# A fused attention and feed-forward layer on 8 cores: the last tile's order of work around its last norm

## The reference

```python
qkv = x @ W_qkv                      # 16 heads of 64
# rotary embedding, windows of 128 tokens that look back one window, causal mask
attn = softmax(mask(q @ k.T)) @ v
x = layernorm(x + attn @ W_out)
gate, up = x @ w_gate.T / 127, x @ w_up.T / 127      # 3072 hidden, int weights
x = layernorm(x + (silu(gate) * up) @ w_down.T / 127)
```

## Time and profile before

| what | value |
|---|---|
| median of 3 runs | 1616.28 us (1616.17 to 1749.54) |
| the profiled execution's own time | 1617.83 us |
| its slowest core, core 7, first to last instruction | 1616.3 us |
| the other cores' spans | 1605.2 to 1614.8 us |
| TensorE busy | 1558.8 us, 96% of the span |
| VectorE, ScalarE, GpSimd busy | 39%, 31%, 14% |
| HBM read / written | 325.19 / 16.78 MB |
| mean granted TensorE clock, core 7 | 0.987 |

### The profile page before, as it was taken

One profiled execution on the slowest core, in us unless ns is written; L12 is line 12 of the kernel. 1 busy time (PEld: TensorE's weight loads), 2 busy tenths in 40 slices (PEclk: granted clock), 3 DMA queues, 4 the chain that ended last, 5 costly groups with the idle time before them and its releaser, 6 DMA issues.

```text
span 1616.3 us, 24558 instructions; the slowest of 8 cores (1605.2 to 1616.3 us)
## 1 busy us (share of the span) xinstructions
PE 1558.8 (96%) x9152; PEld 743.3 (46%) x9152; DVE 624.3 (39%) x1037; ACT 504.2 (31%) x721; POOL 220.2 (14%) x412
## 2 busy tenths in 40 slices
PE   6789999999999999999999999999999999997998
PEld 2344445544454444544445444554445444453443
DVE  0642316522264233632246322562326523363123
ACT  2532224422343223432234222443224422342110
POOL 5112220011100111011110111101120011100100
PEclk9889999999999999999999999999999999999999
DMA  9999995299833989159871798628974299612861
GB/s 152 204 141 182 183 160 101 56 159 160 138 73 72 176 150 156 41 96 174 148 131 37 134 172 142 110 60 137 168 134 92 53 170 162 105 53 46 141 101 52
DMA packets 83635, 198.87 MB, mean 123 GB/s; under 512 B 11712, under 2 KB 20032, under 8 KB 83520
## 3 DMA queue, kind: packets, MB, share of 16 engines
q0 software_dynamic: 64896, 161.51, 64.3%
q1 hardware_dynamic: 18624, 35.81, 6.1%
HBM read 325.19 MB, written 16.78 MB: 212 GB/s over the span
## 4 chain that ended last, share of the span: by engine, by line
PE 90%; DMA 4%; DVE 2%; ACT 2%; issue 1%; POOL 1%; SPq 0%; DVEq 0%; ACTq 0%; POOLq 0%
PE sc L422 40%; PE dn L342 21%; PE dn L391 7%; PE pvb L255 5%; PE dn L255 5%; PE dn L262 3%; PE pvb L262 2%; DMA gu<-wgu_d 2%; DMA h_sb<-wqk_d 2%; PE sc L255 2%; PE sc L303 2%; PE pvb L322 1%; ACT y_fm L550 1%; PE pvb L369 1%; PE sc L262 1%
## 5 line engine op out<-in xcount | busy, mean ns | idle before, releaser
L422 PE MATMUL sc<-y_fm,gu 128*128 128x512 bf16 x2880 | 645.5, 380 | 6.4 <-DMA gu<-wgu_d 4.8
L422 PEld LDWEIGHTS sc<-y_fm,gu 128*128 128x128 bf16 x2880 | 281.5, 98 | 351.0 <-issue 16.3
L753 DVE TENSOR_TENSOR h_sb<-pt,sc 128x512 bf16<-128x512 bf16 x192 | 132.0, 688 | 676.2 <-PE sc L422 628.9
L342 PE MATMUL dn<-wd,h_sb 128*128 128x512 bf16 x1536 | 345.9, 379 | 2.9 <-ACT y_fm L550 2.9
L576 ACT ACTIVATE pt<-sc,consts 128x512 bf16<-128x512 f32 x192 | 131.9, 687 | 321.2 <-PE sc L422 321.1
L342 PEld LDWEIGHTS dn<-wd,h_sb 128*128 128x128 bf16 x1536 | 144.4, 98 | 171.5 <-issue 4.9
L870 POOL DMA_DIRECT2D gu<-wgu_d x180 | 95.2, 529 | 692.5 <-PE sc L422 659.8
L541 ACT ACTIVATE pt<-sc,consts 128x1024 f16<-128x1024 f32 x112 | 129.7, 1202 | 169.4 <-PE sc L303 169.2
L391 PE MATMUL dn<-wo,attn_fm 128*128 128x512 f16 x512 | 117.7, 383 | 2.6 <-ACT attn_fm L546 2.6
L862 POOL DMA_DIRECT2D qk<-wqk_d x112 | 59.8, 538 | 350.9 <-PE sc L255 227.0
L734 DVE SCALAR_TENSOR_TENSOR r<-dn,consts,y_tm 128x512 f32<-128x512 f32 x64 | 48.1, 751 | 128.7 <-PE dn L342 128.7
(11 more groups left out here) (112 smaller groups left out, 1108.1 us busy)
## 6 DMA issues: line engine op xcount, KB each, us to landing
gu<-wgu_d POOLq DMA_DIRECT2D x180, 512.0 KB, 7.1
qk<-wqk_d POOLq DMA_DIRECT2D x112, 256.0 KB, 7.6
out_tm<-r SPq DMA_DIRECT2D x32, 512.0 KB, 2.8
rotb<-qraw SPq DMA_DIRECT2D x232, 64.0 KB, 5.7
x<-x_fm POOLq DMA_DIRECT2D x16, 512.0 KB, 12.9
xt<-x_tm POOLq DMA_DIRECT2D x30, 256.0 KB, 6.5
wd<-wgu_d POOLq DMA_DIRECT2D x12, 512.0 KB, 13.8
wd<-wd_d POOLq DMA_DIRECT2D x24, 256.0 KB, 11.0
```

What stands on the lines that cost most here:

```text
L342: mm = e.matmul(out=bank(D_BANK[p]), lhsT=h_sb[:, hc * TILE + w * 128:hc * TILE + (w + 1) * 128], rhs=wd[:, hc * 1024 + half * 512:hc * 10 ...
L422: mm = e.matmul(out=bank(b0 + part), lhsT=wt[:, part * 1024 + dc * 128:part * 1024 + (dc + 1) * 128], rhs=y_fm[:, dc * TILE:(dc + 1) * TIL ...
L753: e.tensor_tensor(out=h_sb[:, hc * TILE:(hc + 1) * TILE], in0=a_sb[hc % 2], in1=bank(2 * (hc % 2) + 1), op=ALU.mult).then_inc(G["h"], 1)
```

## The change

All of it is in the last tile, `t` = 7. On TensorE the step 7 `down` of tile 6 is cut at 14 and 19 of its 24 matmuls; `pv(t, 7)` goes behind the first part, `transp(t, 3)` and `y_transp(t, 2)` behind the second. Gate/up blocks 0, 1 and 2 are done in two goes: windows 0 to 2 (384 tokens) of blocks 0 and 1 before `y_transp(t, 3)`, of block 2 after it, and then the last 128 tokens of all three. Block 2 uses banks 6 and 7, and the blocks after it swap their pairs of banks. `y_transp(t, 2)` goes to bank 1. ScalarE and VectorE follow this order: `res_2(t-1, 7)` comes after `norm_p(t, 7)`, `final(t-1, 3)` after `y_norm(t, 3)`, and their ScalarE partner `rstd_2(t-1, 3)` after `ty_out(t, 3)`. The weights of blocks 3 to 8 have homes of their own in `x16` and `wv`; POOL issues these six loads behind the tile's last token load, and the ring goes on with block 9, whose load waits for block 0, and so on.

```diff
+def gu_bank(t, hc):
+    if t == NT - 1 and hc >= 2:
+        return 6 if hc == 2 else 2 * ((hc - 1) % 2)
+    return 2 * (hc % 2)
+        gx_home = [x16.ap().bitcast(BF16)[:, i * 2048:(i + 1) * 2048] for i in range(2)]
+        gx_home += [wv.ap().bitcast(BF16)[:, i * 2048:(i + 1) * 2048] for i in range(4)]
+        trbf_last = sc.ap().bitcast(BF16)[:, 1024:2048]
+        def ring(n):
+            return n if n < 24 * (NT - 1) + 9 else n - 6
...
+            def gate_up(t, hc, w0=0, w1=WPT):
                 n = 24 * t + hc
+                b0 = gu_bank(t, hc)
+                if hc == 0 or w0:
+                    e.wait_ge(G["ty_ev"], 4 * t + w1)
                 elif hc >= 2:
-                    e.wait_ge(G["h"], n - 1)
+                    if t == NT - 1 and hc == 2:
+                        e.wait_ge(G["r1"], 8 * t + 8)
+                    else:
+                        e.wait_ge(G["h"], n - 2 if t == NT - 1 and hc < 5 else n - 1)
...
+                elif t == NT - 1 and 3 <= hc < 9:
+                    wt = gx_home[hc - 3]
+                    e.wait_ge(G[f"gx{hc - 3}"], 16)
...
+                                      rhs=y_fm[:, dc * TILE + w0 * 128:dc * TILE + w1 * 128],
                                       start=(dc == 0), stop=(dc == DC - 1))
-                    mm.then_inc(G["g_mm"] if part == 0 else G["u_mm"], 1)
+                    if w1 == WPT:
+                        mm.then_inc(G["g_mm"] if part == 0 else G["u_mm"], 1)
...
                         d_bank_free(t, p)
+                        if p == 7 and t == NT - 1:
+                            down(prev, p, 0, 14)
+                            continue
                         down(prev, p, 0, HC)
...
                 pv(t, 7)
+                if t == NT - 1:
+                    down(prev, 7, 14, 19)
+                    transp(t, 3)
+                    y_transp(t, 2)
+                    down(prev, 7, 19, HC)
+                    outp(t, 3)
+                    gate_up(t, 0, 0, 3)
+                    gate_up(t, 1, 0, 3)
+                    y_transp(t, 3)
+                    gate_up(t, 2, 0, 3)
+                    for hc in range(3):
+                        gate_up(t, hc, 3, 4)
+                    for hc in range(3, HC):
+                        gate_up(t, hc)
+                    continue
...
             def gu_load(n):
+                r = ring(n)
                 if n >= 15:
-                    e.wait_ge(G["u_mm"], n - 2)
+                    e.wait_ge(G["u_mm"], n - 8 if n > r and r < 24 * (NT - 1) + 6 else n - 2)
...
+            def gx_load(i):
+                e.dma_start(out=gx_home[i], in_=wgu_d[3 + i]).then_inc(G[f"gx{i}"], 16)
...
                     for i in range(3, 6):
                         qk_load(t + 1, i)
-                for hc in range(HC - 3):
+                else:
+                    e.wait_ge(G["qk_mm"], 16 * NT)
+                    e.wait_ge(G["v_mm"], 8 * NT)
+                    for i in range(6):
+                        gx_load(i)
+                for hc in range(0 if nxt else 6, HC - 3):
                     gu_load(24 * t + hc + 3)
```

More of the change, by code:

```diff
@@ L171, in build_core_program @@
         names += [f"g0_ld{i}" for i in range(12)]
+        names += [f"gx{i}" for i in range(6)]
         names += [f"rot0_{i}" for i in range(8)] + [f"wv{i}" for i in range(DC)]
@@ L215, in build_core_program, with ty_bank @@
         trbf0 = [sc.ap().bitcast(BF16)[:, 3072:4096]] * 3 + trbf[3:]
+        trbf_last = sc.ap().bitcast(BF16)[:, 1024:2048]
+        def ty_bank(t, w):
+            if t == NT - 1 and w == 2:
+                return trbf_last
+            return trbf[w] if t else trbf0[w]
         cosb = cs[:, 0:TILE].unsqueeze(1).broadcast_to([128, 2, TILE])
@@ L384, in outp @@
                     elif w == 3 and half == 0:
-                        e.wait_ge(G["ty_ev"], 4 * t + w)
+                        e.wait_ge(G["ty_ev"], 4 * t + (w if t < NT - 1 else 2))
+                        if t == NT - 1:
+                            e.wait_ge(G["r1"], 8 * t + 6)
                     elif t:
@@ L399, in y_transp @@
                     e.wait_ge(G["ty_ev"], w)
-                dst = trbf[w] if t else trbf0[w]
+                dst = ty_bank(t, w)
                 for dc in range(DC):
@@ L416, in gate_up @@
                     e.wait_ge(g0_ld[n], 16)
-                else:
-                    wt = gu[n % 3]
-                    e.wait_ge(gu_ld[n % 3], 16 * (n // 3 - 3))
+                elif t == NT - 1 and 3 <= hc < 9:
+                    wt = gx_home[hc - 3]
+                    e.wait_ge(G[f"gx{hc - 3}"], 16)
+                else:
+                    r = ring(n)
+                    wt = gu[r % 3]
+                    e.wait_ge(gu_ld[r % 3], 16 * (r // 3 - 3))
                 for part in range(2):
                     for dc in range(DC):
-                        mm = e.matmul(out=bank(b0 + part),
+                        mm = e.matmul(out=bank(b0 + part)[:, w0 * 128:w1 * 128],
                                       lhsT=wt[:, part * 1024 + dc * 128:part * 1024 + (dc + 1) * 128],
-                                      rhs=y_fm[:, dc * TILE:(dc + 1) * TILE],
+                                      rhs=y_fm[:, dc * TILE + w0 * 128:dc * TILE + w1 * 128],
                                       start=(dc == 0), stop=(dc == DC - 1))
-                    mm.then_inc(G["g_mm"] if part == 0 else G["u_mm"], 1)
+                    if w1 == WPT:
+                        mm.then_inc(G["g_mm"] if part == 0 else G["u_mm"], 1)
             e.wait_ge(G["const"], 16 * 4)
@@ L496, in on_tensor @@
                 pv(t, 7)
-                nxt = t + 1 < NT
-                if nxt:
-                    qkv(t + 1, ORDER[0])
+                if t == NT - 1:
+                    down(prev, 7, 14, 19)
[12 more added lines that the diff above has]
+                    continue
+                qkv(t + 1, ORDER[0])
                 transp(t, 3)
-                if nxt:
-                    qkv(t + 1, ORDER[1])
+                qkv(t + 1, ORDER[1])
                 outp(t, 3)
-                if nxt:
-                    for k in range(2, 5):
-                        qkv(t + 1, ORDER[k])
+                for k in range(2, 5):
+                    qkv(t + 1, ORDER[k])
                 y_transp(t, 3)
-                if nxt:
-                    for k in range(5, LEAD):
-                        qkv(t + 1, ORDER[k])
+                for k in range(5, LEAD):
+                    qkv(t + 1, ORDER[k])
                 for hc in range(HC):
                     gate_up(t, hc)
-                    if nxt and hc in SLOT:
+                    if hc in SLOT:
                         qkv(t + 1, SLOT[hc])
@@ L575, in silu @@
                     e.wait_ge(G["h"], n - 1)
-                e.activation(out=a_sb[hc % 2], in_=bank(2 * (hc % 2)), func=AF.Silu,
+                e.activation(out=a_sb[hc % 2], in_=bank(gu_bank(t, hc)), func=AF.Silu,
                              scale=consts[:, 1:2]).then_inc(G["silu"], 1)
@@ L622, in on_scalar @@
                         rstd_1(t, (p - 3) // 2)
-                        ty_out(t, (p - 3) // 2)
-                if t:
+                        if nxt or p < 7:
+                            ty_out(t, (p - 3) // 2)
+                if nxt:
                     rstd_2(t - 1, 3)
-                if nxt:
                     qkv_out(t + 1, ORDER[0])
                 t_out(t, 3)
+                if not nxt:
+                    ty_out(t, 2)
                 if nxt:
@@ L635, in on_scalar @@
                 ty_out(t, 3)
+                if not nxt:
+                    rstd_2(t - 1, 3)
                 if nxt:
@@ L753, in h_mul @@
                 e.tensor_tensor(out=h_sb[:, hc * TILE:(hc + 1) * TILE], in0=a_sb[hc % 2],
-                                in1=bank(2 * (hc % 2) + 1), op=ALU.mult).then_inc(G["h"], 1)
+                                in1=bank(gu_bank(t, hc) + 1), op=ALU.mult).then_inc(G["h"], 1)
             def carry():
@@ L819, in on_vector @@
                 norm_p(t, 7)
-                if t:
+                if nxt:
                     final(t - 1, 3)
-                if nxt:
                     rope_cos(t + 1, 0)
+                else:
+                    res_2(t - 1, 7)
                 res_1(t, 3, 0)
@@ L828, in on_vector @@
                     rope_sin(t + 1, 0)
+                else:
+                    final(t - 1, 3)
                 for hc in range(HC):
@@ L864, in gu_load @@
             def gu_load(n):
+                r = ring(n)
                 if n >= 15:
-                    e.wait_ge(G["u_mm"], n - 2)
+                    e.wait_ge(G["u_mm"], n - 8 if n > r and r < 24 * (NT - 1) + 6 else n - 2)
                 elif n == 14:
                     e.wait_ge(G["r1"], 8)
-                e.dma_start(out=gu[n % 3][:], in_=wgu_d[n % HC]).then_inc(gu_ld[n % 3], 16)
+                e.dma_start(out=gu[r % 3][:], in_=wgu_d[n % HC]).then_inc(gu_ld[r % 3], 16)
+            def gx_load(i):
```

(1 more changed line is left out.)

9 lines of the change are left out of this document (3 added, 6 removed).

## The result

The changed kernel took 1601.8 us in the median, against the 1604.5 forecast. The ratio to the kernel before is 0.9912 with a 95% interval of 0.9883 to 0.9941; the forecast, 1604.5 / 1616.28, is 0.9927.

The account below looks back on a forecast made before the run. TensorE, 90% of the chain, was taken as the bound, so only its waits and half clock could be won. On core 7, 1616.3 - 10.55 - 1.5 = 1604.2, put at 1604.5 us for two level cores; range 1602 to 1607.

Parts of the forecast that it names:

- the sum: Core 7: 1616.3 less 10.55 up to block 3 and 1.5 of weight waits, 1604.2; with core 4 level, 1604.5 us.
- Steps 1 to 3: Last tile, cut down-projection up to `outp(3)`: waits of 0.2 us before `pv` and 0.3 before `transp`, replacing one of 2.07.
- step 3: Before `outp(3)`: five downs end at 1464.54, `attn_fm` is ready at 1464.53, so no wait and no margin.
- Step 5: 384-token parts of blocks 0 to 2: 0.162 us per matmul, covering the old waits of 3.48 and 1.52 us.
- Step 6: 128-token parts of blocks 0 to 2: 48 matmuls with new weights at 0.057 us each, 2.72 us.
- Step 7: Before block 3: TensorE waits 0.9 us for `h_mul(0)`, behind the table load and first silu.
- The clock: Blocks 0 to 2 of the last tile: half clock after the four waits cost 2.9 us, won if it stays up.
- The weights: Last tile's gate/up blocks: waits for weights fall from 4.8 to 3.3 us, so 1.5 is won.
- the clock falls all the same: Rival, 1460.5 to 1464.5 us: the clock falls once for as long as before, 2.9 us come back, 1607.4; chance 0.09.
- The slower case: Rival: half clock from `pv` to the end of the 128-token parts, +6 us, 1622; chance 0.02.
- the ring as a bound: Rival: weight loads 12 to 23 take 4.2 us each, 4.8 us more of waits, 1609.3; chance 0.12.
- The ring recovers: Rival: only the last few weight loads are late, core 4 keeps 1 us of waits, core 7 none; about 1602; chance 0.11.

Follow-up runs that it names:

- The null run: The kernel before measured against itself, no edit: ratio 1.0001, interval 0.9991 to 1.0010.
- e7: Changed kernel plus a one-column silu on ScalarE in the last tile, so the function table loads before the first gate is ready; ratio to before 0.9908.
- e4: Kernel before plus 38 matmuls whose result nobody reads, put into the last tile's four TensorE waits; ratio to before 0.9971.
- e2: Changed kernel without the six early loads, only the new order, weights through the ring of three; median 1610.7 us, ratio to before 0.9974.
- e10: The changed kernel a third time, no edit, on another chip; median 1603.8 us, ratio to before 0.9927.
- e1: The changed kernel measured again, no edit; median 1601.7 us, ratio to before 0.9923.

## Why the prediction was right or wrong

- *The verdict drawn from the sum was wrong.* The step that failed is in "How the numbers follow": "a measurement of this kernel can tell about 2%, 32 us", and from it "within 2% is nearly sure". A gain of 11.8 us was worked out and then called no change, with 0.97 on "same" and 0.01 on "faster". The ratio did come within 2%, but its interval, 0.9883 to 0.9941, excludes 1. The null run has an interval of 0.1% on either side, the three comparisons of the changed kernel 0.2 to 0.3%. The bound of 2% came from no row: of the three times shown for the kernel before, two were 0.11 us apart, and only the third, 133 us above, is of another kind. Against the two, 11.8 us were clear.
- *Steps 1 to 3, the held-back down-projection: right.* Forecast 0.2 before `pv`, 0.3 before `transp`, start to start; measured 0.17 and 0.34. The margin of zero in step 3 cost 0.2: 1460.33 - 1459.05 is 1.28 instead of 1.08.
- *Step 5, 384 columns: right*, 0.1625 for 0.162. *Step 6, 128 columns: right*, 0.056 for 0.057. The 81 ns that the Trainium skill gives for a 128-column matmul with its weight load ("TensorE: Matmul & The Clock Gate", Back-to-back issue gap) do not hold in this stretch.
- *Step 7, the new wait before block 3: right* in place and cause (e7 took it away), and 1.15 start to start instead of 0.9.
- *The clock: right mechanism, sized from one core.* I read 2.9 us on core 7. Over the cores it is 3.2, and 5.0 on core 4, which was only 1.5 us behind: I took it for a second bound and gave it too small a gain. e4 shows the clock alone to be worth 4.7 us in the total, 2.6 to 6.6. For core 7 itself my reading was 0.2 too high: the issue follows block 2's end by 0.71, not 0.5, which makes it 2.7, and the forecast of 10.55 a 10.35.
- *The weights: right in the price, wrong in what it means.* On the slowest core B to E was 1551.70 - 1475.87 = 75.83, so 3.3 of waits, as forecast. But the means are 2.3 before and 1.6 after, so the ring's part of the gain is 0.7 and not 1.5; core 7 of the profiled execution, with 4.8 up to block 20, was the extreme. And the early loads are worth 8 us to the new order (e2), which the sum, with the two as separate terms, did not say.
- *Rivals.* Where the rival "the clock falls all the same" looked, between `pv` and block 3, the clock stayed at 1.00 on all 24 cores of the changed kernel. But on core 7 of e10 it fell later, in one wait for weights, which neither the forecast nor a rival had (its timeline, and the window behind the wait):

```profile
1518.18 36.74 PE L456 MATMUL sc<-y_fm,gu 128*128 128x512 bf16 x160 [2.23 <-DMA gu<-wgu_d]
1519.00:1522.00 3.00, 3.00 (x8) 1.06 (x7) 0.00 (x0) 0.69 (x1) 0.00 (x0) 0.50 0.87 154
```

  That core has the longest S to E of the three executions, 99.7 us. The slower case and the ring as a bound did not come. "The ring recovers" gave about 1602, which is what was measured, but not by its mechanism: the slowest core still had 3.3 us of waits, and they went only with nine buffers.
- *The sum: near in part by luck.* B comes 10.3 us sooner after S on average (10.55 forecast), E 10.9 (12.05 forecast), and the total is 12 to 14 us less. Between the slowest cores of the two profiled executions, 1616.3 and 1600.3 us, 11.6 us lie in S to E and 4.4 before S, where nothing was changed but the issue of the early loads. The slowest core deciding is not the reason: in the medians over e10's executions the slowest core is 11.7 us shorter than before and the mean of all eight 11.5, in e1 13.9 and 12.9. Where the 1 to 2 us beyond S to E come from is not shown.

## What to carry to other kernels

Size a term on every core that is within reach of the slowest, not on the slowest alone, and hold the sum against the scatter of the runs themselves before calling it no change. When a reordering makes several consumers of a short buffer ring end together, their reloads are asked for together too: look for idle buffers to load ahead, or the wait only moves, and takes the half clock with it. Work placed into a wait pays twice where the wait had let the clock fall.

## What the runs showed of the hardware

- Matmuls that compute nothing useful, put into 8.4 us of waits, made the program 0.29% faster (0.16% to 0.41%); 3.2 us of it can be seen in the trace, where the granted clock stayed at 1.00.
- Where the clock falls differs from core to core within one execution: in the first of the four waits (core 6, 2.07 us), the second (core 4) or only the fourth (core 7). Single waits for weights among dense blocks went either way: it fell in one of 2.23 us (e10, core 7) and stayed at 1.00 in one of 2.10 (e7, core 1).
- DMA in the last tile carried a load of 512 KB each 3.45 us on all eight cores once nine could be in hand; the landing time of one (8.5 to 23.4 us for the six early loads issued together, core 5 of the changed kernel) says nothing of whether it can.
